# Opening of the state-space stage: GpSimd's products after the normalised rows, TensorE's turning and projecting interleaved with dummy matmuls, single waits for the first coefficients

## The reference

```python
x = x + _L0_attn_ref(_layernorm(x, axis=-1), ...)
...
proj = jnp.einsum('btd,od->bto', x, W_in)          # gate, value_raw, params (32 heads x 2)
dt = jnp.clip(jax.nn.softplus(params[..., 0] + dt_bias), DT_MIN, DT_MAX)
kd = K_MAX * jax.nn.sigmoid(params[..., 1])
A = jnp.exp(A_log)
...
def step(carry, inp):
    S = 1.0 / (1.0 + dt_t[..., None] * k_t[..., None] + (dt_t * dt_t)[..., None] * A)
    z = S[..., None] * (z - dtE * A[None, :, :, None] * s + dtE * (Bz_t[..., None] * u_t[:, :, None, :]))
    s = s + dtE * z + dtE * (Bx_t[..., None] * u_t[:, :, None, :])
```

## Time and profile before

| what | value |
|---|---|
| median of 3 runs | 1362.73 us (1361.03 to 1363.33) |
| profiled execution, time on the device | 1364.74 us |
| its span, first to last instruction | 1363.0 us |
| TensorE busy | 1271.2 us (93%) |
| VectorE busy | 913.2 us (67%) |
| ScalarE busy | 637.4 us (47%) |
| GpSimd busy | 587.3 us (43%) |
| mean granted clock of TensorE | 0.981 |

### The profile page before, as it was taken

The page is one execution under the profiler, slowest core; times in us unless marked ns, Lnnn a source line. Parts: engine busy times, 40 slices in busy tenths (PEclk is TensorE's granted clock), DMA queues, the critical chain, the costliest instruction groups (busy, mean ns, idle before and its releaser), DMA issues. The chain is left out here.

```text
span 1363.0 us, 22827 instructions
## 1 busy us (share of the span) xinstructions
PE 1271.2 (93%) x7784; PEld 706.3 (52%) x7784; DVE 913.2 (67%) x1773; ACT 637.4 (47%) x1537; POOL 587.3 (43%) x939
## 2 busy tenths in 40 slices
PE   4999757999999999999799998999999999899999
PEld 3443224566566556666445545555555556454545
DVE  6999996989998989898310304888787787630100
ACT  2265313555565565565322314666565576632221
POOL 2633313788878888888300001444444444410000
PEclk9999978999999999999799999999999999999999
DMA  2257897555555655556200002000000000000000
GB/s 81 124 231 322 309 388 260 187 186 182 187 189 182 202 178 188 194 190 209 89 1 0 0 0 88 1 1 1 1 2 1 1 1 1 1 1 0 16 0 16
DMA packets 67714, 143.51 MB, mean 105 GB/s; under 512 B 6800, under 2 KB 22800, under 8 KB 64784
## 3 DMA queue, kind: packets, MB, share of 16 engines
q1 hardware_dynamic: 62992, 129.47, 26.9%
q10 hardware_dynamic: 4608, 12.58, 2.3%
HBM read 94.58 MB, written 47.45 MB: 104 GB/s over the span
## 5 line engine op out<-in xcount | busy, mean ns | idle before, releaser
L1755 POOL TENSOR_SCALAR pr<-pr,rs,sg 128x512 f32<-128x512 f32 (+3 forms) x256 | 151.9, 608 | 208.0 <-DVE rs L1657 208.0
L595 PE MATMUL banks<-w_bc,valueT 128*128 128x512 f32 x448 | 212.0, 597 | 2.4 <-ACT own L889 1.6
L954 DVE TENSOR_TENSOR pp<-banks,rec 128x1024 f32<-128x1024 f32 x128 | 156.2, 1220 | 8.2 <-DMA dd<-det 2.2
L1568 ACT ACTIVATE pr<-banks,nm 128x512 f32<-128x512 f32 (+3 forms) x256 | 132.5, 523 | 25.4 <-DVE nm L1651 22.8
L595 PEld LDWEIGHTS banks<-w_bc,valueT 128*128 128x128 f32 x448 | 77.4, 192 | 60.2 <-issue 57.3
L1651 DVE TENSOR_REDUCE nm<-banks 128x2 f32<-128x1024 f32 (+3 forms) x128 | 105.6, 825 | 4.4
L1036 POOL TENSOR_SCALAR_AFFINE_SELECT bp<-bp 128x1024 f32<-128x1024 f32 x64 | 73.5, 1148 | 77.7 <-ACT bp L843 77.6
L1292 DVE TENSOR_TENSOR x<-x,banks 128x256 f32<-128x256 f32 x16 | 6.7, 422 | 148.3 <-PE banks L1203 148.3
L305 DVE TENSOR_TENSOR X<-X,banks 128x256 f32<-128x256 f32 x256 | 105.5, 494 | 0.0
L1556 ACT COPY prT<-banks 128x512 f32<-128x512 f32 (+3 forms) x128 | 54.2, 423 | 109.3 <-PE banks L1452 109.1
L836 ACT COPY qk<-banks 128x512 f32<-128x512 f32 x128 | 74.9, 585 | 64.2 <-PE banks L723 64.2
(11 more groups left out here) (237 smaller groups left out, 2443.3 us busy)
## 6 DMA issues: line engine op xcount, KB each, us to landing
rec<-psi SPq DMA_DIRECT2D x128, 512.0 KB, 4.5
psi<-X SPq DMA_DIRECT2D x15, 2048.0 KB, 7.4
det<-w_bc ACTq DMA_DIRECT2D x16, 512.0 KB, 4.9
dd<-det SPq DMA_DIRECT2D x64, 128.0 KB, 4.6
bcs<-pre ACTq DMA_DIRECT2D x16, 256.0 KB, 7.6
w_bc<-in_w_bc SPq DMA_DIRECT2D x4, 1024.0 KB, 10.6
back<-bcs SPq DMA_DIRECT2D x16, 256.0 KB, 5.1
w_bc<-in_f_h SPq DMA_DIRECT2D x4, 1024.0 KB, 8.1
```

What stands on the lines that cost most here:

```text
L595: mm = pe.matmul(bank, m["valueT"][:, c, t * P:(t + 1) * P], w, start=(c == 0), stop=(c == 1))
L954: dve.tensor_tensor(pp[:, q % 2].rearrange("p (a c) n -> p a c n", c=2), sc.unsqueeze(2).broadcast_to([P, 4, 2, HN]), rec[:, n % RL, q % 2 ...
L1568: act.activation(pr[:, n % RP, h, 0:w], S[n % 2][:, h, 0:w], ACT.Exp, bias=nm[:, n % 4, h:h + 1], accum_out=sm[:, m % 3, n % 2, h:h + 1]). ...
L1755: pool.tensor_scalar(row, row, rs[:, n // 2 % 2, n % 2, h:h + 1], sg[:, TPB * b + it, hd:hd + 1], ALU.mult, ALU.mult).then_inc(s["scaled"], 1)
```

## The change

Three edits in `front`:

1. GpSimd waits for all sixteen `xn` before AB and `wk` (one added wait).
2. TensorE's opening is written batch by batch: `turn_rows(b)` transposes the four tiles of a batch, `project_rows(b)` multiplies the four tiles with the parameter columns, one batch behind. Ahead of it stand three matmuls of one triangle of ones with the other over 512 columns, and after it four more (`warm`). They write bank 7, which L338's matmul overwrites later; nothing reads what they leave.
3. VectorE no longer waits for all eight coefficients of block 0; the product with C of step q waits for q + 1 of them. Later blocks wait as before.

```diff
--- before.py
+++ after.py
@@ -283,7 +283,8 @@
             dve.wait_ge(s["abT_ready"], 2)
             for i in range(NBLK):
                 r = i % RINGX
-                dve.wait_ge(s["alpha"], STEPS * (i + 1))
+                if i > 0:
+                    dve.wait_ge(s["alpha"], STEPS * (i + 1))
                 if i >= RINGX:
                     dve.wait_ge(stored[r], 16 * (i // RINGX))
                 for q in range(STEPS):
@@ -293,6 +294,8 @@
                     for n, a in enumerate(order):
                         if j > 0:
                             dve.wait_ge(rec, 4 * (j - 1) + 3 + n)
+                        if i == 0 and a == 1:
+                            dve.wait_ge(s["alpha"], q + 1)
                         if a == 0:
                             dve.tensor_tensor(T2[:, n].rearrange("p c (h n) -> p c h n", n=N),
                                               BETA[:, :, j].unsqueeze(1).unsqueeze(3).broadcast_to([P, 2, G4, N]),
@@ -321,19 +324,35 @@
         @block.tensor
         def _(pe):
             pe.wait_ge(s["consts"], 3)
-            for t in range(TILES):
-                pe.wait_ge(s["xn"], t + 1)
-                pe.transpose(k.bank[t // TPB][:, t % TPB * P:(t % TPB + 1) * P], xn[:, t, :],
-                             k.ident[:]).then_inc(s["xnT_ready"], 1)
-            pe.wait_ge(s["w_loaded"], 16)
-            for t in range(TILES):
-                if t % TPB == 0:
-                    pe.wait_ge(s["xnT_taken"], t // TPB + 1)
-                b, lo = t // TPB, PAD + t % TPB * P
-                mm = pe.matmul(DKB[t // 8][:, t % 8 * PCOL:(t % 8 + 1) * PCOL], xp[:, b, lo:lo + P],
-                               w_in[:, DI:DI + PCOL])
-                if t % 8 == 7:
+
+            def warm(n):
+                for _ in range(n):
+                    pe.matmul(LPB[:], ones_lt[:], ones_le[:].unsqueeze(1).broadcast_to([P, TPB, P]))
+
+            def turn_rows(b):
+                for t in range(b * TPB, (b + 1) * TPB):
+                    pe.wait_ge(s["xn"], t + 1)
+                    pe.transpose(k.bank[b][:, t % TPB * P:(t % TPB + 1) * P], xn[:, t, :],
+                                 k.ident[:]).then_inc(s["xnT_ready"], 1)
+
+            def project_rows(b):
+                pe.wait_ge(s["xnT_taken"], b + 1)
+                for t in range(b * TPB, (b + 1) * TPB):
+                    lo = PAD + t % TPB * P
+                    mm = pe.matmul(DKB[t // 8][:, t % 8 * PCOL:(t % 8 + 1) * PCOL], xp[:, b, lo:lo + P],
+                                   w_in[:, DI:DI + PCOL])
+                if b % 2 == 1:
                     mm.then_inc(s["dk_ready"], 1)
+
+            warm(3)
+            for b in range(B):
+                turn_rows(b)
+                if b == 1:
+                    pe.wait_ge(s["w_loaded"], 16)
+                if b > 0:
+                    project_rows(b - 1)
+            project_rows(B - 1)
+            warm(4)
             pe.wait_ge(s["lf"], 1)
             pe.matmul(LPB[:], ones_lt[:], lf).then_inc(s["LF"], 1)
             pe.matmul(LFB[:], ones_le[:], lf).then_inc(s["LF"], 1)
@@ -535,6 +554,7 @@
                                    ALU.add).then_inc(s["em"], 1)
             pool.wait_ge(s["em"], 3)
             pool.wait_ge(s["aexp"], 2)
+            pool.wait_ge(s["xn"], TILES)
             pool.tensor_tensor(AB[:], alog[:].unsqueeze(1).broadcast_to([PCOL, H, N]),
                                emask[:].unsqueeze(2).broadcast_to([PCOL, H, N]), ALU.mult).then_inc(s["AB"], 1)
             pool.wait_ge(s["AB"], 1)
```

## The result

The changed kernel takes 1355.7 us, the median of six runs (1353.94 to 1358.1), the kernel before beside it 1363.03 (1360.31 to 1365.16): a ratio of 0.9941, 95% interval 0.9924 to 0.9957, 7.3 us less by the medians. The forecast was 1355.2 from 1362.73, 7.5 less. The profiled execution has 1357.57 us and a span of 1355.8, forecast 1357.2 and 1355.5.

A forecast was written before the change was run, and what follows sets the result against it. The prediction took VectorE's unbroken recurrence, hence the waits before step 0, as the bound. Gains of 3.9 us (opening) and 3.6 us (sums to step 0) made 7.5: 1362.73 to 1355.2 us, range 1351.0 to 1359.0.

The forecast's parts named there:

- What bounds: First stage: VectorE's unbroken recurrence, 1.34 us a step, so the stage's end moves with step 0's start at 39.24 us.
- GpSimd behind the rows: Opening: without GpSimd's jobs beside them, the second eight rows take 2.14 us instead of 5.83, ending 3.69 us earlier.
- Turning and projecting: TensorE's opening: batchwise transposes and projections end at 20.1 us instead of 23.97, 3.9 us gained.
- The clock of the opening: TensorE's opening runs at the lower level, 1.2 GHz, so projection records stay 0.217 us each.
- rival 1: Opening at full clock: projections and transposes end about 15.8 us, 3.6 more gained in all, 1351.6; chance 0.17.
- The first three dummies: Ahead of the transposes: take 5.1 us, over at 7.4 before the first row; reaching the higher level left open.
- The four behind and the reciprocal: After the projections: dummies end at 25.9 to 26.7, sums run warm; the reciprocal hides half a us of lateness.
- From the sums to step 0: L338's start to step 0: 5.6 us instead of 9.19, 3.6 gained, 2.4 by single waits and 1.2 by clock.
- Does the wait cost a step?: Recurrence's first steps beside GpSimd's coefficients: 0.2 us lost over five steps, at most 0.1 more than before.
- TensorE's list behind: TensorE's work after step 0's start: moves 7.5 us earlier like VectorE, 2.2 of them from convolution at full clock.
- the sign I named: Convolution on TensorE: its first records would lie 0.43 us apart.
- Rivals 3 and 4: Stage's tail: late stores eat the gain, 1362, chance 0.06; or psi stores behind two more prepared stores, 1372, chance 0.04.

The follow-up runs named there:

- the held clock: Changed kernel with four dummies ahead instead of three, plus one after every second transpose of the first two batches: median 1354.44 us, ratio 0.9916.

## Why the prediction was right

- **What bounds.** Right for the changed kernel. The stage's end moved 7.75 us for 7.3 of step 0, and next to nothing moved behind it (1147.5 against 1147.0). In six of the experiments' profiles TensorE's list was last instead.
- **GpSimd behind the rows.** Right: 2.14 us for the second eight. Its 3.69 us are not a term of their own, though; taken back alone they cost 1.8.
- **Turning and projecting.** Right: 11.0 us behind the first row, worked out 20.1 - 8.6 = 11.5; with the later input 3.6 of the span's us, 4.4 by distance.
- **The clock of the opening.** The choice, the projections at 0.22, held in the profile. What I took from it was too much: the row before shows unbroken projections that never reach the higher level, and I let that stand for every execution. In four of the experiments' profiles and in the changed kernel's second they did, halfway. So rival 1 was not an alternative but a part that some executions get, 1.4 us of it, and holding the clock gets 3.3.
- **The first three dummies** raised the clock and lost it before use. They bring nothing that these runs can show, and may cost the halfway rise.
- **The four behind and the reciprocal.** Right: ends at 26.44 (25.9 to 26.7 forecast), sums at the higher level, L271 straight behind the reciprocal. Taking them out costs 0.8 to 1.5 us; 1.2 were forecast.
- **From the sums to step 0.** 31.92 - 26.47 = 5.45, worked out 5.6. Single waits are worth 2.7 us, put at 2.4.
- **Does the wait cost a step?** No: four steps took 5.32 us, 1.33 each, so not even the 0.2 came. GpSimd paid instead: its sixteen coefficients took 7.21 us, before 6.64. The Trainium skill (SBUF — State Buffer, "Who interferes with whom") would have a product with two inputs in SBUF blocked by a GpSimd instruction that reads there. Beside the coefficients of 0.41 us most rows don't show it: L304 took 0.42 in the changed kernel, though the first one took 0.63 without dummies and 0.58 with the held clock. Beside pf, 1.03 us long, it took 0.97 instead of 0.42, and there the trace agrees.
- **TensorE's list behind.** The step that failed. I had it gain 7.5 us, 2.2 of them by starting the convolution at full clock. In the first profile it started slow again, so that the sign I named (first records 0.43 apart) didn't show, and the gate's matmuls began at 63.70 instead of 68.22, 4.5 earlier. In the second it did start at full clock and the gate began at 58.67, 9.6 earlier by distance from the first row. Neither carried through to the list's end, 173.1 us behind step 0 in the first profile and 175.1 in the second, before 174.9. In between the list waits for stores; that this sets its end is read from the traces, no run isolates it. I also took the slack for 1.9 us where it was 0.7. The changed kernel had 2.1 in one profile and 0.1 in the other, so that this error stayed out of the sum is partly luck.
- **How near the number came** is partly luck too. By distance from the first row step 0 gained 8.1 us in one profile and 9.5 in the other, not 7.5. The first row itself came at 8.60 in the profile before and at 8.62 to 9.64 in the others, and the interval of the ratio reaches from 5.9 to 10.4 us gained, so it can't tell 7.5 from 9.
- **Rivals 3 and 4** describe something real: 6.9 us in the list cost 3.9, and one execution lost 9 us by late stores, the determinants' first. In no median did it come.

## What to carry to other kernels

Two remedies for one gap don't add: cost each with the other in place (here 1.8 and 0.7 us, together 4.4). Dummy matmuls paid here only where the clock was still up when the critical matmuls came, so put them directly ahead of those, or fill the thin stretch as well; a raised clock during work that waited for another engine was worth nothing. After moving a chain's start, compare the slack of every stream that ends near the same barrier, and take off the time that the barrier itself needs: here 2.1 us in one execution and 0.1 in another.

## What the runs showed of the hardware

The clock's rise in a stretch of dense work differs from one execution to the next: the same sixteen projection records took 3.51 us in the changed kernel's first profile and 2.07 in the second. The granted clock reads 1.00 at the very start although the six records there take 5.49 us, which is 0.85 apart, the spacing of the lower level; only the lengths tell. And a VectorE multiplication with both inputs in SBUF took 0.42 to 0.63 us beside GpSimd products of 0.41, while those grew to 7.21 us for sixteen, and 0.97 us beside one of 1.03.
